# A graph layer with linear attention and experts: order of norm, sums and weight splits in the mix stage

## The reference, cut to what matters

```
xn  = layernorm(x)
x1  = x + xn @ Wg.T + gnn_bias + (attention(xn) @ W_out + b_out)
      Wg: dense 1024x1024 matrix, scatter-add of 41250 weighted edges
      attention: linear, 16 heads, q and k RMS-normed, scaled, relu
x2  = layernorm(x1)
t   = x2 * rsqrt(mean(x2*x2) + 1e-5) * norm_scale
y   = sum over the top 2 of 8 experts (router: t @ gate_w + gate_b)
      of prob * (swiglu(t @ w1 + b1) @ w2 + b2)
out = x1 + x2 + y
```

## Time and profile before

| | |
|---|---|
| median of 3 runs | 1023.72 us (1021.45 to 1023.92) |
| profiled execution, own time | 1024.34 us |
| its span, first to last instruction | 1022.6 us |
| PE busy | 924.6 us, 90% |
| DVE busy | 709.8 us, 69% |
| ACT busy | 366.9 us, 36% |
| POOL busy | 174.1 us, 17% |
| DMA into `arena` from `in_w_flat`, share of the chain of waits | 7% |

### The profile page before, as it was taken

One profiled execution on the slowest core, in us unless ns is written; L12 is line 12 of the kernel. 1 busy time (PEld: TensorE's weight loads), 2 busy tenths in 40 slices (PEclk: granted clock), 3 DMA queues, 4 the chain that ended last, 5 costly groups with the idle time before them and its releaser, 6 DMA issues.

```text
span 1022.6 us, 16194 instructions
## 1 busy us (share of the span) xinstructions
PE 924.6 (90%) x5355; PEld 578.3 (57%) x5356; DVE 709.8 (69%) x1200; ACT 366.9 (36%) x621; POOL 174.1 (17%) x210
## 2 busy tenths in 40 slices
PE   5887999999999999998999999998359999999993
PEld 3555667677765654555666666665335454555551
DVE  5777999999999974378767777755545555555551
ACT  5648666665531124431112212222113332333331
POOL 1000000000000000015223222322122233323322
PEclk9998999999999999998999999999569999999996
DMA  9643667666652009910255556566459968886544
GB/s 311 223 137 131 202 215 220 195 189 211 205 191 104 22 22 262 315 42 1 61 165 151 158 159 163 154 168 181 163 215 311 308 172 254 266 251 142 123 82 62
DMA packets 89162, 176.59 MB, mean 173 GB/s; under 512 B 24824, under 2 KB 39160, under 8 KB 89088
## 3 DMA queue, kind: packets, MB, share of 16 engines
q1 hardware_dynamic: 81328, 147.50, 46.0%
q0 software_dynamic: 7776, 28.32, 12.4%
HBM read 113.63 MB, written 62.67 MB: 172 GB/s over the span
## 4 chain that ended last, share of the span: by engine, by line
PE 42%; DVE 18%; DMA 18%; ACT 6%; issue 6%; POOL 4%; SPq 3%; DVEq 0%; POOLq 0%; ACTq 0%
PE bank L765 10%; PE windows L1041 9%; PE bank L915 7%; DMA arena<-in_w_flat 7%; DMA arena<-t_dram,arena 6%; PE bank L1059 4%; DMA split_dram<-arena 2%; DVE arena L1696 2%; POOL arena L656 2%; PE bank L1032 2%; SPq L542 2%; PE windows L797 2%; DVE arena L1520 2%; DMA out_x<-arena 1%; PE windows L798 1%
## 5 line engine op out<-in xcount | busy, mean ns | idle before, releaser
L765 PE MATMUL bank<-arena 128*125 128x512 f16 x960 | 217.3, 384 | 8.7 <-DVE arena L1488 4.8
L765 PEld LDWEIGHTS bank<-arena 128*125 128x125 f16 x960 | 130.6, 138 | 82.5 <-DVE arena L1488 5.6
L1041 PE MATMUL windows<-arena 128*128 x648 | 149.2, 380 | 0.0
L915 PE MATMUL bank<-arena 128*128 128x416 f16 (+1 forms) x576 | 107.9, 343 | 2.0 <-DMA arena<-split_dram 2.0
L941 PE MATMUL bank<-arena 128*125 128x512 f16 x432 | 97.6, 383 | 4.1 <-DVE arena L1732 2.5
L1041 PEld LDWEIGHTS windows<-arena 128*128 128x128 f16 x648 | 63.6, 98 | 65.4 <-issue 1.0
L947 PE MATMUL bank<-arena 128*125 128x512 f16 x432 | 98.4, 386 | 0.0
L915 PEld LDWEIGHTS bank<-arena 128*128 128x128 f16 x576 | 55.7, 98 | 47.0 <-issue 3.0
L941 PEld LDWEIGHTS bank<-arena 128*125 128x125 f16 x432 | 59.4, 138 | 38.9 <-issue 3.7
L1758 DVE SCALAR_TENSOR_TENSOR arena<-arena 128x512 f16<-128x512 f32 x40 | 39.9, 999 | 59.7 <-ACT arena L1330 59.6
L947 PEld LDWEIGHTS bank<-arena 128*125 128x125 f16 x432 | 60.2, 139 | 35.0 <-issue 2.6
(11 more groups left out here) (250 smaller groups left out, 1425.0 us busy)
## 6 DMA issues: line engine op xcount, KB each, us to landing
arena<-split_dram SPq DMA_DIRECT2D x56, 512.0 KB, 5.7
arena<-in_w_flat SPq DMA_DIRECT2D x44, 512.0 KB, 4.4
split_dram<-arena SPq DMA_DIRECT2D x88, 256.0 KB, 4.6
arena<-in_w_flat SPq DMA_DIRECT2D x40, 256.0 KB, 4.3
split_dram<-arena SPq DMA_DIRECT2D x80, 128.0 KB, 2.3
arena<-in_x SPq DMA_DIRECT2D x20, 448.0 KB
arena<-in_w_qkv SPq DMA_DIRECT2D x8, 1024.0 KB, 10.7
t_dram<-arena SPq DMA_DIRECT2D x10, 448.0 KB
```

The source lines that it names most:

```text
L765: mm = pe.matmul(bank[b][0:TT, :], xt[:, l, k, tok(i)], wkv[:, r, k, c0:c0 + 512], start=(k == 0 and n == 0), stop=(k == KT - 1 and n == 2))
L915: mm = pe.matmul(bank[u % 3][:, 0:n], wq[h][:, l, k, :], xt[:, r, k, a:a + n], start=(k == 0 and c == 0), stop=(k == KT - 1 and c == 2))
L1041: mm = pe.matmul(bank[6][:, :], rowT[s][:, l, k, :], arena16[:, bass.ds(off + (r * KT + k) * 512, 512)], start=(k == 0 and c == 0), stop=( ...
```

## The change

Three things are reordered; no instruction is added or removed.

- SP: for each quarter piece q, the request of piece q+2 is issued before the two stores of piece q instead of after them.
- DVE, tiles 2 to 7: `mix_norm(i-1)` and `gate(i-3)` come before unit 0; Q1 and Q2 both come ahead of unit 2; the residual sums stand right behind units 2 and 3; Q3 and Q4 come last.
- ACT, tiles 2 to 7: `mix_sqrt(i-1)` before the first `attend_hi`, and the splits in the same places as on DVE.

```diff
             def next_quarters(qs):
                 for q in qs:
                     sp.wait_ge(quarter_lo, q + 1)
+                    if q + 2 < QUARTERS:
+                        quarter_ask(q + 2)
                     for hl in range(2):
                         sp.dma_start(quarter_rows(split_dram[hl], q), quarter_part[q % 2][:, hl, :]).then_inc(quarter_out[q % 2], 16)
-                    if q + 2 < QUARTERS:
-                        quarter_ask(q + 2)
...
             for i in range(2, NT - 2):
                 t, h = divmod(i, 2)
                 qs = list(quarters(i))
-                attend_hi(4 * h, t + 1, PAIRS * (t + 1) + 4 * h)
                 mix_sqrt(i - 1, 1 - h)
-                for j in range(1, 4):
-                    quarter_split(qs[j - 1])
+                for j, some in enumerate((qs[0:1], qs[1:3], [], qs[3:])):
                     attend_hi(4 * h + j, t + 1, PAIRS * (t + 1) + 4 * h + j)
-                for q in qs[3:]:
-                    quarter_split(q)
+                    for q in some:
+                        quarter_split(q)
                 tt_copy(i - 1)
...
                 qs = list(quarters(i))
-                attend_unit(4 * h, t + 1, unit)
                 mix_norm(i - 1, (i - 1) // 2, 1 - h)
                 if i > 2:
                     gate(i - 3)
+                attend_unit(4 * h, t + 1, unit)
                 quarter_split(qs[0])
                 attend_unit(4 * h + 1, t + 1, unit + 1)
-                quarter_split(qs[1])
+                for q in qs[1:3]:
+                    quarter_split(q)
                 attend_unit(4 * h + 2, t + 1, unit + 2)
-                quarter_split(qs[2])
                 add_half(i, h, 0)
                 attend_unit(4 * h + 3, t + 1, unit + 3)
-                quarter_split(qs[3])
                 add_half(i, h, 1)
-                for q in qs[4:]:
+                for q in qs[3:]:
                     quarter_split(q)
```

## The result

| | before | changed |
|---|---|---|
| median | 1022.59 us (1021.18 to 1023.92, 4 runs) | 1035.43 us (1030.97 to 1036.34, 4 runs) |
| profiled execution, own time | 1024.34 us | 1036.34 us |

The ratio is 1.0108, 95% interval 1.007 to 1.0146: slower, by 12.8 us in the medians (1.0126 as their plain ratio, inside the interval) and 12.0 in the profiled executions. The forecast was 1037 for the median and 1037.8 for the profiled execution.

A forecast was written before the change was run, and what follows sets the result against it. The mix stage's loop over VectorE, GpSimd, SP and a DMA was taken as the bound; +3.66 and -0.94 made its step 29.68 against 26.96. With start and last tiles, +13.5 us: 1037 us median, range 1026 to 1044.

The forecast's parts named there:

- What bounds the stage: Mix stage, tiles 3 to 7: a loop over VectorE, GpSimd, SP and a DMA, 26.96 us a tile.
- Norm first, +3.66: GpSimd's mix_out, queued behind its part of unit 0, starts 8.37 us after the norm in place of 4.71.
- Request ahead, -0.94: Q2's request gains the two stores' data time, 0.94 us, landing 7.03 after the base store in place of 7.97.
- slower still: Rival: stores put behind the request hold ScalarE, landing 8.8, 1.8 us more in eight tiles, 1051 us; chance 0.07.
- Unit 2 behind Q2, +2.52 and -2.52: VectorE: unit 2 now waits for Q2, costing 2.52 us, against 2.52 that unit 0 leaves at the loop's end.
- Q4 held by mix_in: End of tile: GpSimd's mix_in holds Q4's split, so the next norm comes 3.29 us after mix_in's start.
- Tile 2's L1750: Norm's last VectorE operation in tile 2, meeting mix_in: costs 0 if it passes, 2.1 us if held; 1.1 taken.
- Step and sum: Step by tile 29.68 us against 26.96; tile 7's norm at 686.6, last norm at 725.1, +13.5 us in all.
- Faster: Rival: request lands 3.9 us after the base store, step 26.6, TensorE binds in tile 7, 1020 us; chance 0.06.
- No change: Rival: landing at 5.0, step 27.7, 1025 us; or Q4 not held by mix_in, 1026; together chance 0.12.
- unheld Q4: Second form of no change: mix_in doesn't hold Q4's split, five tiles at 2.2 us less, 1026 us.

The follow-up runs named there:

- e1: Kernel before with only SP's order changed, request of piece q+2 ahead of piece q's two stores: 1010.11 us, ratio 0.9875 to before; timed again 1015.06 us, 0.9927.
- e3: Changed kernel with mix_out moved ahead of the low part of unit 0 on GpSimd: 1012.08 us, ratio 0.9900 to the kernel before.
- e4: Changed kernel with Q2's split put behind unit 2 again on VectorE and ScalarE: 1021.77 us, ratio 0.9995 to the kernel before.
- e5: Changed kernel with GpSimd's mix_in adding the bias to 8 of 1024 columns only: 1024.76 us, ratio 1.0030 to the kernel before.
- e7: Changed kernel with mix_out ahead of unit 0's low part and Q2's split behind unit 2: 1015.06 us, ratio 0.9935 to the kernel before.
- e6: Changed kernel with three output buffers for split quarters in place of two: 1028.54 us, ratio 1.0068 to the kernel before.

## Why the prediction was right, step by step

- **What bounds the stage.** Right: a loop over VectorE, GpSimd, SP and a DMA. Four edits at four places of it (e1, e3, e4, e5) each moved the step, and near TensorE's pace the gain stopped: e1 and e3 leave it no wait beyond 0.54 us, and in e7 VectorE and ScalarE alone need 25.13.
- **Norm first, +3.66.** Right. mix_out starts 8.35 behind the norm (8.37 forecast), behind a GpSimd operation that the diff doesn't show, and e3 takes that away by a move on GpSimd alone.
- **Request ahead, -0.94.** This term was mis-sized: ScalarE's split gains 1.4 us in either order (7.87 to 6.44, 7.83 to 6.45). That the stores ahead of the read count, and not the time of issue, was right, as e3 shows (issued at 2.01, landed at 5.61). The price was wrong: 256 KB over 280 GB/s is 0.94 us, and the read gained 2.3 (7.85 to 5.56). 280 GB/s in the earlier trace rows went with a DMA share of 0.80, so it doesn't show a full queue; why two stores cost a read over 2 us stays open. The second thing missing is that the stores then hold ScalarE, 0.9 us beyond the read (e6), which gives part of it back; this was in the rival "slower still", but at 6.4 and not at 8.8. Two errors of opposite sign left 0.5, which is luck. The term was off by 0.58 us (7.03 less 6.45) a tile, 2.7 us over the five steps (29.68 less 29.14).
- **Unit 2 behind Q2, +2.52 and -2.52.** Right; e4 finds 2.84.
- **Q4 held by mix_in.** Right: 3.49 us for the pair, the norm 3.27 behind mix_in's start (3.29), and e5 shows the cause.
- **Tile 2's L1750 (now L1748).** I took the middle of 0 and 2.1. It was held in full, as the second of these rows ends at 510.17:

```profile
508.10 3.15 DVE L1748 SCALAR_TENSOR_TENSOR arena<-arena 125x1024 f32<-125x1024 f32 x1
...
507.72 2.45 POOL L652 TENSOR_TENSOR arena<-arena 125x1024 f32<-125x1024 f32 x1 [2.50 <-DMA arena<-in_x]
```

Its 3.15 us are 1.9 more than the 1.29 of e5. The Trainium skill's rule on two SBUF inputs ("SBUF — State Buffer", "Who interferes with whom") would have given the right end. With the landing's error the other way (6.42 us in tile 2, not 7.03), the norm in tile 3's program starts at 538.27, where 538.2 was forecast: the two errors cancel, by luck.

- **Step and sum.** 29.14 against 29.68, by the landing. The norms of the rows of tiles 7, 8 and 9, then the step of the last one that waits for ScalarE's square root:

```profile
683.95 0.68 DVE L1734 BATCH_NORM_STATS2 arena<-arena 125x6 f32<-125x512 f32 x1
...
704.92 0.69 DVE L1734 BATCH_NORM_STATS2 arena<-arena 125x6 f32<-125x512 f32 x1
...
722.18 0.69 DVE L1734 BATCH_NORM_STATS2 arena<-arena 125x6 f32<-125x512 f32 x1
...
725.14 0.16 DVE L1739 RECIPROCAL arena<-arena 125x1 f32<-125x1 f32 x1 [1.32 <-ACT arena L1316]
```

683.95 (686.6 forecast), then 20.97 (21.2) and 17.26 (17.3). The last is 10.6 us behind the 711.57 of before, where 13.5 was forecast, and 1 us is lost behind it (1.32 us of waiting in place of 0.36): its square root stands in ScalarE's order behind the copy of tile 8's transposes. That gives 11.6 of the 12.0; the rest lies in the later stages. The prediction didn't have this 1 us, and without it the time would be 2.9 us off and not 1.5.
- **The rivals.** "Faster" needed a landing below 4.9; the shortest of the changed kernel is 5.99. "No change" by a landing of 5.0: 5.5 is reached only with a third buffer, and by an unheld Q4: not so here, but e5 at 1024.76 bears out its price. The base store weighed against "faster" is 500 KB in two transfers and not 448; at 280 GB/s that is 1.8 us in place of 1.6, which changes nothing.

## What to carry to other kernels

When work is reordered on one engine, follow each result to the engine that takes it, and look at what stands ahead of it in that engine's own order: here the norm was put ahead of unit 0, and GpSimd, whose order stayed, couldn't take its result before unit 0's. Write the stage's binding loop as a sum from one trace and check that it gives the measured step; then each edit is a term, and a good edit (request first) can be told from the two bad ones in the same change. Test parts alone: this change held a gain of 1.2% (0.9875) and a loss of 2.4% (1.0108 / 0.9875); the order alone measured 1.0212.

## What the runs showed of the hardware

- A 256 KB read issued ahead of two 128 KB stores landed 5.56 us behind the base store (mean of eight tiles of the changed kernel), and 7.85 behind the stores (before). Issued at 2.01 us in place of 0.81, but still ahead of the stores, it landed at 5.61 (e3): the place in the order counted, not the 1.2 us.
- The two stores, issued 1.0 and 1.5 us behind such a read, landed last some 0.9 us after it (the split starts at 6.45, and at 5.53 without them, e6), so the order read-then-stores moves the wait from the read to the stores.
- A GpSimd `tensor_tensor` of 2.8 us holds a VectorE operation with two SBUF inputs until its end: 2.1 us for a 128x512 split (e5), 1.9 for the 125x1024 L1748.
- It goes the other way too: mix_out takes 2.79 us where VectorE's split of 0.73 us started 0.14 ahead of it (changed kernel), and 2.35 where none runs at its start (e3).
